# Payload swaps of a bitonic sort in a graph kernel: predicated copies in place of a difference, with ScalarE keeping the old half

## The reference

```python
edge_index = jnp.stack([src, dst])
h = jnp.maximum(_layernorm(x, axis=-1), 0.0)
for _ in range(3):
    hh, t = agg[head], agg[tail]
    att = jnp.sum((hh @ q_w) * jnp.tanh(rel * t @ k_w), axis=1)
    e = jnp.exp(att - segment_max(att, head)[head])
    w = e / segment_sum(e, head)[head]
    summed = segment_sum(w[:, None] * rel * t, head)
    agg = summed / jnp.maximum(cnt, 1.0)[:, None]
    agg = agg / jnp.maximum(norm(agg), 1e-12)
    out = out + agg + entity_emb
```

## Time and profile before

| | us |
|---|---|
| median of 3 runs | 2251.78 |
| lowest and highest run | 2236.15, 2257.71 |
| the profiled execution's own time | 2228.32 |
| its span, first to last instruction | 2226.2 |
| VectorE busy | 1316.6 (59%) |
| GpSimd busy | 1219.3 (55%) |
| TensorE busy | 1074.8 (48%) |
| ScalarE busy | 802.1 (36%) |

### The profile page before, as it was taken

How to read it: one execution, slowest core, us unless ns; L and a number is a source line. 1 busy time by engine, 2 the same in 40 slices (tenths; PEclk the granted TensorE clock), 3 DMA queues, 4 the chain that set the end, 5 groups by cost and what they waited for, 6 DMA issues and landing times. The chain is left out here.

```text
span 2226.2 us, 22847 instructions
## 1 busy us (share of the span) xinstructions
PE 1074.8 (48%) x5076; PEld 876.2 (39%) x5076; DVE 1316.6 (59%) x5932; ACT 802.1 (36%) x2503; POOL 1219.3 (55%) x1218
## 2 busy tenths in 40 slices
PE   0010133333359554675421666878545469777420
PEld 0000122222248443465320445768534348577320
DVE  8888675555653445635841654383756453688970
ACT  0000055555733454523631431271643222524420
POOL 1000455555655666763777777620037676567776
PEclk9999986666655766655555886785767677855555
DMA  8800344444432323313542764530269897657771
GB/s 228 237 8 0 133 142 161 163 154 159 144 97 84 94 87 100 118 64 104 177 156 87 220 196 127 141 124 34 83 166 193 148 181 145 166 159 205 212 207 35
DMA packets 194443, 302.78 MB, mean 136 GB/s; under 512 B 31284, under 2 KB 113536, under 8 KB 189652
## 3 DMA queue, kind: packets, MB, share of 16 engines
q1 hardware_dynamic: 154460, 202.55, 28.0%
q0 software_dynamic: 38400, 72.99, 16.0%
q10 hardware_dynamic: 1448, 25.80, 4.2%
HBM read 175.78 MB, written 130.86 MB: 138 GB/s over the span
## 5 line engine op out<-in xcount | busy, mean ns | idle before, releaser
L550 POOL DMA_INDIRECT tr<-in_x_dram,tidx x200 | 193.8, 969 | 425.7 <-DVEq L778 236.2
L1322 PE MATMUL ps<-rt,wr 128*125 128x128 f32 x1200 | 264.9, 395 | 262.2 <-DVE wr L935 153.3
L1259 PE MATMUL ps<-ident,rt 128*128 128x128 f32 x600 | 129.3, 354 | 456.3 <-DVE rt L997 429.9
L1322 PEld LDWEIGHTS ps<-rt,wr 128*125 128x125 f32 x1200 | 235.2, 293 | 285.3 <-DVE wr L935 171.5
L550 POOL DMA_INDIRECT tr<-agg_d,tidx x200 | 198.6, 993 | 256.1 <-issue 236.8
L1148 ACT ACTIVATE sqj<-ps,invc 125x128 bf16<-125x128 f32 x600 | 213.7, 380 | 289.7 <-PE ps L1322 289.7
L1259 PEld LDWEIGHTS ps<-ident,rt 128*128 128x128 f32 x600 | 88.9, 182 | 483.1 <-DVE rt L997 451.1
L1107 ACT COPY rtT<-ps 128x512 f32<-128x512 f32 x150 | 87.8, 586 | 489.5 <-PE ps L1259 489.5
L562 POOL DMA_INDIRECT ntab_d<-rt,lidx x200 | 209.8, 1049 | 95.7 <-issue 59.3
L562 POOL DMA_INDIRECT out_dram<-rt,lidx x200 | 211.5, 1057 | 89.2 <-issue 60.3
L550 POOL DMA_INDIRECT tr<-ntab_d,tidx x200 | 197.2, 986 | 67.6 <-issue 59.4
(11 more groups left out here) (222 smaller groups left out, 2228.7 us busy)
## 6 DMA issues: line engine op xcount, KB each, us to landing
agg_d<-rt SPq DMA_DIRECT2D x100, 258.0 KB, 2.4
xr<-agg_d SPq DMA_DIRECT2D x100, 258.0 KB, 3.8
relr<-rel_d SPq DMA_DIRECT2D x100, 256.0 KB, 4.2
ntab_d<-rt ACTq DMA_DIRECT2D x15, 1679.7 KB
rt<-in_x_dram SPq DMA_DIRECT2D x13, 1024.0 KB, 6.6
out_dram<-rt SPq DMA_DIRECT2D x13, 1024.0 KB, 4.0
acc_d<-xr SPq DMA_DIRECT2D x50, 258.0 KB, 2.9
rel_d<-relr SPq DMA_DIRECT2D x50, 256.0 KB, 2.3
```

The source lines that it names most:

```text
L550: G.indirect_dma_start(out=row, out_offset=None, in_=table[:, :], in_offset=bass.IndirectOffsetOnAxis(ap=idx[:, n:n + 1], axis=0)).then_in ...
L1259: ins = T.transpose(ps[B_TR][:, t, :], rt[:, g * GT + t, 0:D], ident[:, :])
L1322: ins = T.matmul(ps[B_T + j % 2][0:R, t, :], wr[:, (j % 2) * GT + t, 0:R], rt[:, j * GT + t, 0:D], start=True, stop=True)
```

## The change

Four things change.

1. In a step of the sort the payload is swapped by two predicated copies. The comparison goes to PSUM (two banks in turn). ScalarE copies the lower payload half to `vold` ahead of the swap; then `va` takes `vb` where the comparison is true, and `vb` takes `vold` there. The first copy waits for ScalarE (`s_vc`), the second for the first (`s_vx`); ScalarE's copy of the next step waits for both. Five VectorE instructions and one of ScalarE stand where seven of VectorE stood.
2. The signs of two successive merges are multiplied beforehand, so that one pass stands ahead of each merge. The products are made before the inputs are waited for.
3. A turn is split: TensorE transposes the keys and reports (`s_xp`), then waits for the last payload swap and transposes the payload (`s_xv`); ScalarE copies the payload out of PSUM, VectorE only the keys.
4. The tile of zeros has 1075 columns in place of 5375. Each of the 15 DMAs reads it five times over: 400 rows of 1075 elements (4,300 B) in place of 80 rows of 5375 (21,500 B).

```diff
-ZP, ZC = 80, 5375
+ZP, ZC, ZR = 80, 5375, 1075
...
-        zeros = upper[0:ZP, 0:ZC]
+        zeros = upper[0:ZP, 0:ZR]
...
+        SORT = []          # (k, m, payload copies done before the step)
...
-            dve.wait_ge(s_ld, 16 * 3)
-            ch.note(V.tensor_copy(kbuf[0], raws[0]))
-            ch.note(V.scalar_tensor_tensor(vbuf, raws[1], float(NREL), raws[2], ALU.mult, ALU.add))
             dve.wait_ge(s_const, 11)
             for k in range(8):
                 ch.note(V.tensor_scalar(pbits[:, k:k + 1], pbits[:, 8:9], k, 1, ALU.logical_shift_right, ALU.bitwise_and))
+            ch.note(V.tensor_copy(sgn7, sgn[7]))
             ch.join()
-            ch(V.tensor_scalar(sgnp[:, 0:8], pbits[:, 0:8], -2.0, 1.0, ALU.mult, ALU.add))
+            ch.note(V.tensor_scalar(sgnp[:, 0:8], pbits[:, 0:8], -2.0, 1.0, ALU.mult, ALU.add))
+            for k in range(7, 1, -1):
+                ch(V.tensor_tensor(sgn[k], sgn[k], sgn[k - 1], ALU.mult))
+            ch(V.tensor_tensor(signs[:, 1:7], sgnp[:, 1:7], sgnp[:, 0:6], ALU.mult))
+            dve.wait_ge(s_ld, 16 * 3)
+            ch(V.tensor_copy(kbuf[0], raws[0]))
+            V.scalar_tensor_tensor(vbuf, raws[1], float(NREL), raws[2], ALU.mult, ALU.add).then_inc(s_vb, 1)
...
-                ch.note(V.tensor_tensor(m, ka, kb, ALU.is_gt))
-                ch.note(V.tensor_tensor(d, vb, va, ALU.subtract))
+                ch.note(V.tensor_tensor(gt, ka, kb, ALU.is_gt))
                 ch.note(V.tensor_tensor(na, ka, kb, ALU.min))
-                dve.wait_ge(s_dve, ch.at - 1)
-                ch.note(V.tensor_tensor(d, d, m, ALU.mult))
                 ch.note(V.tensor_tensor(nb, ka, kb, ALU.max))
-                dve.wait_ge(s_dve, ch.at - 1)
-                ch.note(V.tensor_tensor(va, va, d, ALU.add))
-                ch(V.tensor_tensor(vb, vb, d, ALU.subtract))
+                dve.wait_ge(s_vc, step + 1)
+                dve.wait_ge(s_dve, ch.at - 2)
+                V.copy_predicated(va, gt.bitcast(I32), vb).then_inc(s_vx, 1)
+                dve.wait_ge(s_vx, n + 1)
+                V.copy_predicated(vb, gt.bitcast(I32), old).then_inc(s_vx, 1)
+                ch.join()
...
-                apply_sign(kbuf[at], k - 1)
-                apply_sign(kbuf[at], k)
+                apply_signs(kbuf[at], k)
...
-                    ch.note(V.tensor_copy(kT[bt], bank(0)[:, 0:SC]))
-                    ch(V.tensor_copy(vT, bank(1)[:, 0:SC]))
+                    ch(V.tensor_copy(kT[bt], bank(0)[:, 0:SC]))
...
+            dve.wait_ge(s_vx, 2 * len(SORT))
             dve.sem_inc(s_go, 1)
...
@@ ScalarE
             for z in range(NZ):
-                act.dma_start(zt[z], zeros).then_inc(s_z, 16)
+                act.dma_start(zt[z].rearrange("p (k c) -> p k c", c=ZR), zeros.unsqueeze(1).to_broadcast([ZP, ZC // ZR, ZR])
+                              ).then_inc(s_z, 16)
             act.wait_ge(s_qT, 1)
             A.copy(qwT[:, 0:D], ps[7][:, 0, :]).then_inc(s_qTs, 1)
+            act.wait_ge(s_vb, 1)
+            turns = 0
+            for step, (k, m, n) in enumerate(SORT):
+                v, low = (vT, 8) if m > 7 else (vbuf, 0)
+                if k > 8 and m in (k - 1, 7):
+                    turns += 1
+                    act.wait_ge(s_xv, turns)
+                    A.copy(v, bank(1)[:, 0:SC]).then_inc(s_vl, 1)
+                    act.wait_ge(s_vl, turns)
+                elif n > 0:
+                    act.wait_ge(s_vx, n)
+                stride = 1 << (m - low)
+                A.copy(vold.rearrange("p (n s) -> p n s", s=stride),
+                       v.rearrange("p (n t s) -> p n t s", t=2, s=stride)[:, :, 0, :]).then_inc(s_vc, 1)
...
@@ TensorE
                     for c in range(2):
-                        T.transpose(ps[0][:, c, :], kk[:, c * P:(c + 1) * P], ident[:, :])
+                        ins = T.transpose(ps[0][:, c, :], kk[:, c * P:(c + 1) * P], ident[:, :])
+                    ins.then_inc(s_xp, 1)
+                    pe.wait_ge(s_vx, payload_at[i + 9, i + 8 if way == 0 else 7][1])
+                    for c in range(2):
                         ins = T.transpose(ps[1][:, c, :], vv[:, c * P:(c + 1) * P], ident[:, :])
-                    ins.then_inc(s_xp, 1)
+                    ins.then_inc(s_xv, 1)
```

More of the change, by code:

```diff
@@ L197, in gnn_kernel @@
         vT = flat[:, 5 * SC:6 * SC]
-        swapm = flat[:, 6 * SC:6 * SC + 128]
-        swapd = flat[:, 7 * SC:7 * SC + 128]
+        vold = flat[:, 6 * SC:6 * SC + 128]
+        signs = flat[:, 7 * SC:7 * SC + 9]
+        sgn7 = flat[:, 49 * SC:50 * SC]
         raws = [flat[:, (8 + i) * SC:(9 + i) * SC].bitcast(I32) for i in range(3)]
@@ L256, in gnn_kernel @@
         s_srt = sem("s_srt")
+        s_vx = sem("s_vx")
+        s_vc = sem("s_vc")
+        s_xv = sem("s_xv")
+        s_vb = sem("s_vb")
+        s_vl = sem("s_vl")
         s_xp = sem("s_xp")
@@ L308, in gnn_kernel @@
         s_pace = sem("s_pace")
+        SORT = []
+        done = 0
+        for k in range(1, LOGN + 1):
+            for m in range(k - 1, 7, -1):
+                SORT.append((k, m, done + 2 * (k - 1 - m)))
+            done += 2 * max(k - 8, 0)
+            for m in range(min(k, 8) - 1, -1, -1):
+                SORT.append((k, m, done + 2 * (min(k, 8) - 1 - m)))
+            done += 2 * min(k, 8)
+        payload_at = {(k, m): (i, n) for i, (k, m, n) in enumerate(SORT)}
         block = ctx.enter_context(nc.Block())
@@ L711, in exchange, with apply_signs @@
                 va, vb = halves(v)
-                m = swapm.rearrange("p (n s) -> p n s", s=stride)
-                d = swapd.rearrange("p (n s) -> p n s", s=stride)
-                ch.note(V.tensor_tensor(m, ka, kb, ALU.is_gt))
-                ch.note(V.tensor_tensor(d, vb, va, ALU.subtract))
+                step, n = payload_at[k, m]
+                gt = bank(2 + step % 2)[:, 0:128].rearrange("p (n s) -> p n s", s=stride)
+                old = vold.rearrange("p (n s) -> p n s", s=stride)
+                ch.note(V.tensor_tensor(gt, ka, kb, ALU.is_gt))
                 ch.note(V.tensor_tensor(na, ka, kb, ALU.min))
-                dve.wait_ge(s_dve, ch.at - 1)
-                ch.note(V.tensor_tensor(d, d, m, ALU.mult))
                 ch.note(V.tensor_tensor(nb, ka, kb, ALU.max))
-                dve.wait_ge(s_dve, ch.at - 1)
-                ch.note(V.tensor_tensor(va, va, d, ALU.add))
-                ch(V.tensor_tensor(vb, vb, d, ALU.subtract))
-            def apply_sign(t, k):
-                if 1 <= k < 8:
-                    ch(V.tensor_tensor(t, t, sgn[k], ALU.mult))
-                elif 8 <= k < LOGN:
-                    ch(V.tensor_scalar(t, t, sgnp[:, k - 8:k - 7], None, ALU.mult))
+                dve.wait_ge(s_vc, step + 1)
[4 more added lines that the diff above has]
+                ch.join()
+            def apply_signs(t, k):
+                if k == 1:
+                    ch(V.tensor_tensor(t, t, sgn[1], ALU.mult))
+                elif k < 8:
+                    ch(V.tensor_tensor(t, t, sgn[k], ALU.mult))
+                elif k == 8:
+                    ch(V.scalar_tensor_tensor(t, t, sgnp[:, 0:1], sgn7, ALU.mult, ALU.mult))
+                elif k < LOGN:
+                    ch(V.tensor_scalar(t, t, signs[:, k - 8:k - 7], None, ALU.mult))
+                else:
+                    ch(V.tensor_scalar(t, t, sgnp[:, LOGN - 9:LOGN - 8], None, ALU.mult))
             at, hand = 0, 0
             for k in range(1, LOGN + 1):
-                apply_sign(kbuf[at], k - 1)
-                apply_sign(kbuf[at], k)
+                apply_signs(kbuf[at], k)
                 if k > 8:
@@ L739, in _ @@
                     bt = (k - 8) % 2
-                    ch.note(V.tensor_copy(kT[bt], bank(0)[:, 0:SC]))
-                    ch(V.tensor_copy(vT, bank(1)[:, 0:SC]))
+                    ch(V.tensor_copy(kT[bt], bank(0)[:, 0:SC]))
                     for m in range(k - 1, 7, -1):
-                        exchange(kT[bt], kT[1 - bt], vT, 1 << (m - 8))
+                        exchange(k, m, kT[bt], kT[1 - bt], vT, 1 << (m - 8))
                         bt = 1 - bt
@@ L747, in _ @@
                     dve.wait_ge(s_xp, hand)
-                    ch.note(V.tensor_copy(kbuf[0], bank(0)[:, 0:SC]))
-                    ch(V.tensor_copy(vbuf, bank(1)[:, 0:SC]))
+                    ch(V.tensor_copy(kbuf[0], bank(0)[:, 0:SC]))
                 for m in range(min(k, 8) - 1, -1, -1):
-                    exchange(kbuf[at], kbuf[1 - at], vbuf, 1 << m)
+                    exchange(k, m, kbuf[at], kbuf[1 - at], vbuf, 1 << m)
                     at = 1 - at
             assert at == 0
+            dve.wait_ge(s_vx, 2 * len(SORT))
             dve.sem_inc(s_go, 1)
```

2 lines of the change are left out of this document (1 added, 1 removed).

## The result

The changed kernel takes 2280.53 us (median of 19 runs, 2259.84 to 2293.0) where the kernel before takes 2249.5 (median of 19, 2226.35 to 2260.17) beside it. The ratio is 1.0145, with a 95% interval of 1.0121 to 1.0169: slower by some 33 us, where 46 us faster was forecast. The end of this document has a version at 0.974.

The account below looks back on a forecast made before the run. The prediction took VectorE's chain in the sort, the whole kernel's head start, as the bound. 61.3 us saved on VectorE less a 15.1 us stall gave 46 us, from 2251.8 to 2206 us; range 2180 to 2262.

Parts of the forecast that it names:

- the sort is the head start: Whole kernel: GpSimd's first gather waits 236.2 us for the sort, so a microsecond off it comes off the end.
- VectorE's sum: VectorE in the sort: step, signs, turns and start together save 61.3 us, between 22 and 77.
- The step at 1.12 to 1.15: Sort step, 120 times: 1.12 us reckoned, 1.15 taken, in place of 1.54; saves 46.8 us.
- The sign passes: Signs ahead of the merges: two passes ran 14 times each, eight and seven are left; saves 5.5 us.
- term for the start: Before the first sign pass: it starts at 11.7 us, not 12.28; saves 0.6, between -1 and 1.5.
- the turns: Transposes in the sort, 14 times: each 0.6 us shorter, saving 8.4 us; bounds 4 and 10.8.
- ScalarE's copy stays covered: Sort step: ScalarE's copy of the old half takes 0.66 us with hand-offs, VectorE returns at 0.80; covered by 0.14.
- The comparison in PSUM: Sort step: comparison and masks in PSUM cost nothing extra; by the skill's cycles the step would save 31 us, not 47.
- The formula of the stall: First predicated copy, once: VectorE waits 15c - 2.9 us behind ScalarE's 15 DMA issues; 15.1 us taken.
- c itself: Time of one zero-writing DMA issue on ScalarE: 1.2 us taken, bounds 0.32 and 12.7.
- the held-by-rows case: Rival, ScalarE's issues: 6,000 rows hold it until about 105 us; stall 94, loss 33, 2285 us; chance 0.16.
- point of decision (c = 4.3): ScalarE's issues: from 4.3 us an issue on, the stall reaches the 61.3 us saved on VectorE.

Follow-up runs that it names:

- zeros_sync: The changed kernel with its 16 zero-writing DMAs issued by SyncE, behind the input loads, in place of ScalarE; 2194.76 us, ratio 0.9741 to the kernel before.

## Why the prediction was wrong

- **That the sort is the head start**, and that a shift of its end reaches the end of the kernel: right. For the kernels with several runs every shift of the first gather comes back in the ratio within about 10 us.
- **VectorE's sum**: 61.3 us forecast, 55.5 measured, and 55.9 in zeros_sync, where no stall is mixed in. The step at 1.12 to 1.15 was right for 78 steps (1.13) and wrong for the 42 with short runs (1.32), so the steps gave some 41 us in place of 46.8; that is the whole difference. The sign passes gave the 5.5 forecast (2.4 us of gather and 3.1 of products; the prediction counts the products in its term for the start). The start gave 0.9 in place of 0.6. What is left for the turns is some 8.5, with 8.4 forecast. ScalarE's copy stays covered in the steps.
- **The comparison in PSUM** cost next to nothing, as forecast: with the mask in PSUM or in SBUF the copies differ by 1 ns and the first gathers by 0.7 us; the comparison itself takes 308 ns into PSUM and 291 into SBUF, and no later instruction waits for the difference. The reading behind it was weak, though. It set a copy with one source out of PSUM (0.42 us) beside a pass with two sources in SBUF (425 ns); the pass with one source in SBUF took 353. By the Trainium skill ("VectorE: DVE Perf Modes", section on the TRN2 errata) PSUM sources cost more fixed cycles, an estimated 0.13 us a step or 16 us in all; for these masks the trace does not agree.
- **The formula of the stall**, 15c - 2.9: right. The issues took 80.6 us, which makes c 5.37 and the stall 77.7; it measured 78.0.
- **The step that failed is c itself**, 1.2 us taken, 5.4 measured. Two readings went wrong. I took the issue's time for two packets' time, because the one was twice the other in one place; the third to fifth issues took as long with packets a fifth the size, so c would have been near 2.5 even without a hold. And I set the held-by-rows case at 0.16 because 512 rows were issued in 0.62 us: that shows that rows cost little to issue, and says nothing of how many may wait. Before, at most some 900 had waited in this queue (1,460 packets issued, 582 landed by 50 us); 6,000 were asked for, and the long holds began when some 1,550 waited. The rival was priced at a release at 105 us and 2285; the release came at 88.7, and the median is 2280.5. Its mechanism, its place and its point of decision (c = 4.3) were right; the chance given to it was not. That its 2285 came so close to 2280.5 is in part luck: its stall of 94 was 16 too long and its gain of 61.3 on VectorE 6 too much, and some 10 us of the measured loss are not explained by the first gather.

The Trainium skill ("DMA: Bandwidth & Descriptors", section "Issuing engines are not separate DMA queues") says that the time to initiate a DMA on the sequencer is usually small beside the DMA itself. The traces here do not agree: an issue took 2.3 to 3.0 us without a hold and up to 11.8 with one, where one DMA's 1.7 MB moved in an estimated 6.5 us (21.07 MB in the 79 us to the release). What helps is that the issuing engine can be chosen: on SyncE 90 us of issues cost nothing.

## What to carry to other kernels

An engine that starts to feed the critical chain inherits everything that stands ahead of it in its own stream; look there for DMA issues first, since their time appears as idle time that nobody waited for. Cutting a source tile and repeating it in the access pattern multiplies the rows in the queue, and a queue that is full holds the engine that issues: count rows times DMAs before. A place in the trace that shows an issue to be cheap says nothing of the state in which the queue was never seen.

## What the hardware showed

- On one queue the sixth issue of 400 rows of 4,300 B, with some 1,550 packets waiting, took 9.7 us, and the fifth of 400 rows of 12,900 B, with as many waiting, took 21.3. Issues from the third on took 2.0 to 3.9 us without such a hold, whether of 80 or 400 rows and of 4,300, 12,900 or 21,500 B; the first two, and one of 1,200 rows alone, took 0.3 to 0.7. It is no fixed number of packets that decides: with about 1,100 waiting one issue took 2.60 us and a later one 5.03, and ScalarE was released with 1,484, 1,164 and 795 waiting.
- A predicated copy of 128 columns takes 0.29 to 0.30 us, and 0.43 to 0.44 when its destination lies in runs of one or two f32 elements; the read side and the mask's memory make no difference.
- The length of the hold scatters: 80.6 and 88.5 us for the same issues in two executions of the same kernel, with the transfers under 2 us apart.
